# A two-layer decoder on one core: the first loads issued inside the first projection

## What is computed

```python
Q = x @ Wq; K = x @ Wk; V = x @ Wv          # 16 heads of 16
Q = _rope(Q, cos2, sin2); K = _rope(K, cos2, sin2)
scores = where(causal, Q @ K.T / 4, -inf)
x = _layernorm(x + softmax(scores) @ V @ Wo)
```

## Time and profile before

| | us |
|---|---|
| median of 3 runs | 1048.94 (1048.7 to 1051.43) |
| profiled execution | 1048.75 |
| span of the profiled execution | 1047.0 |
| mean granted clock of TensorE | 0.89 of full speed |

### The profile page before, as it was taken

One profiled execution on the slowest core, in us unless ns is written; L12 is line 12 of the kernel. 1 busy time (PEld: TensorE's weight loads), 2 busy tenths in 40 slices (PEclk: granted clock), 3 DMA queues, 4 the chain that ended last, 5 costly groups with the idle time before them and its releaser, 6 DMA issues. The chain is left out here.

```text
span 1047.0 us, 16284 instructions
## 1 busy us (share of the span) xinstructions
PE 842.6 (80%) x4838; PEld 498.2 (48%) x4838; DVE 625.5 (60%) x1971; ACT 439.3 (42%) x1422; POOL 433.7 (41%) x343
## 2 busy tenths in 40 slices
PE   1959998577475699889999998995994499999920
PEld 0445556344254344355555554883444355555510
DVE  0369994566558477668888887113665633433427
ACT  0038782355156100078888886001112155555512
POOL 0348871244026066556666664000000455565523
PEclk9989998677579699989999999998995599999975
DMA  9200000000000077620000000005911022222114
GB/s 349 108 1 1 0 1 1 0 2 1 0 1 1 17 164 171 141 81 1 2 1 2 1 1 1 1 1 212 317 74 40 16 63 71 73 69 70 51 57 144
DMA packets 30974, 60.44 MB, mean 58 GB/s; under 512 B 6465, under 2 KB 20429, under 8 KB 30032
## 3 DMA queue, kind: packets, MB, share of 16 engines
q1 hardware_dynamic: 17424, 35.99, 10.8%
q10 hardware_dynamic: 8864, 13.00, 4.4%
q0 software_dynamic: 4608, 10.50, 3.2%
HBM read 40.59 MB, written 8.39 MB: 47 GB/s over the span
## 5 line engine op out<-in xcount | busy, mean ns | idle before, releaser
L534 POOL TENSOR_TENSOR a_Pr<-a_Pr,a_rd 128x1024 f32<-128x1024 f32 x64 | 121.3, 1895 | 68.0 <-DVE a_rd L475 67.7
L507 ACT ACTIVATE a_Pr<-a_Sm,a_nm 128x257 f32<-128x257 f32 x256 | 127.3, 499 | 34.2 <-DVE a_nm L459 33.4
L459 DVE CUSTOM_DVE_ANT_0 a_Sm<-a_psS,table,NSK 128x256 f32<-128x256 f32 x256 | 107.7, 477 | 1.8 <-PE a_psS L408 1.8
L408 PE MATMUL a_psS<-KT,QT 64*128 64x256 f32 x512 | 74.2, 410 | 5.7 <-DVE a_nm L459 3.8
L1427 POOL TENSOR_TENSOR ro_in_tile<-ro_in_tile,table 128x384 fp32r<-128x384 f32 x4 | 7.0, 1746 | 173.0 <-DVE ro_in_tile L1486 173.0
L1597 POOL DMA_INDIRECT pairs<-ex_y,ti_index x48 | 49.6, 1034 | 57.5 <-ACT ex_y L1702 56.9
L1110 PE MATMUL p_ps<-p_XT,W 128*128 128x512 f32 x160 | 72.6, 612 | 0.8 <-ACT p_XT L1123 0.8
L408 PEld LDWEIGHTS a_psS<-KT,QT 64*128 64x128 f32 x512 | 45.3, 190 | 57.9 <-issue 48.6
L1140 DVE SCALAR_TENSOR_TENSOR p_T<-p_ps,BQK,table 128x512 f32<-128x512 f32 x80 | 56.4, 746 | 26.7 <-PE p_ps L1110 26.7
L1720 DVE TENSOR_TENSOR ex_a<-ex_psG,ex_sg 128x96 f32<-128x96 f32 x48 | 12.4, 258 | 99.9 <-ACT ex_sg L1690 99.9
L421 PE MATMUL a_psT<-table,a_Pr 128*128 128x128 f32 x512 | 70.8, 282 | 1.5 <-ACT a_PT L514 1.5
(11 more groups left out here) (265 smaller groups left out, 2001.2 us busy)
## 6 DMA issues: line engine op xcount, KB each, us to landing
w_in<-in_w_in SPq DMA_DIRECT2D x1, 6144.0 KB, 18.3
QT<-p_E SPq DMA_DIRECT2D x64, 64.0 KB, 2.1
QT<-p_E ACTq DMA_DIRECT2D x64, 64.0 KB, 2.1
c_in<-in_c_in SPq DMA_DIRECT2D x1, 4096.0 KB, 29.2
co_G<-pairs SPq DMA_DIRECT2D x8, 512.0 KB, 7.5
W<-in_w ACTq DMA_DIRECT2D x1, 3072.0 KB, 16.6
w_out<-in_w_out SPq DMA_DIRECT2D x1, 3072.0 KB, 43.0
KT<-p_E SPq DMA_DIRECT2D x32, 64.0 KB, 2.1
```

The costliest lines, as they stand in the source:

```text
L408: last = nc.tensor.matmul(psS[:, 2 * (t % 2) + u, qt, :], heads.q(g, n, qt), heads.k(g, n), start=True, stop=True, skip_group_check=True)
L459: nc.vector.tensor_tensor_reduce(out=Sm[:, t % 2, n, 0:S], in0=psS[:, 2 * (t % 2) + n // 2, n % 2, :], in1=mask[:, n % 2, :], scale=-scale ...
L507: nc.scalar.activation(Pr[:, t % 4, n, :], src, ACT.Exp, bias=nm[:, t % 2, n:n + 1], scale=scale if mask is None else -1.0, accum_out=den[ ...
L534: pool.tensor_tensor(p, p, rd[:, t % 2, :].unsqueeze(2).to_broadcast([P, 4, S]), ALU.mult).then_inc(normed, 1)
```

## The change

The loading block is gone. ScalarE issues the three parts of `W0` as its first instructions in the block of `project_0`, and SyncE issues all other loads in the same block, in the order of their first use: `XT`, table, `WU`, `WD`, `X`, `WO0`, `CTX`, `CT`, `HAD`, `TOK`, `GM`, `SK`, `BO1`, `W1`. The loads themselves, their sizes and the semaphores are the same.

```diff
-def project_0(nc, c, XT, W0, QT, KT, V, WU, WD, ternary, loads):
+def project_0(nc, c, XT, W0, QT, KT, V, WU, WD, ternary, loads, load_w0, load_rest):
...
         jobs = [(a, half, n) for a in range(2) for half in range(KD) for n in range(2)]
+
+        @block.sync
+        def _(sp):
+            load_rest(sp)
...
         @block.scalar
         def _(act):
+            load_w0(act)
             for t in range(NT):
                 act.wait_ge(v_made, t + 1)
...
-                with nc.Block() as block:
-                    @block.sync
-                    def _(sp):
-                        xTs = xT.rearrange("(k p) s -> p k s", p=P)
...
-                    @block.scalar
-                    def _(act):
-                        for n, m in (("q", slice(0, 2)), ("k", slice(2, 4)), ("v", slice(4, 5))):
...
+                def load_w0(act):
+                    for n, m in (("q", slice(0, 2)), ("k", slice(2, 4)), ("v", slice(4, 5))):
+                        act.dma_start(W0[:, m], w0[m].rearrange("m (k p) o -> p m k o", p=P)
+                                      ).then_inc(loads["w0" + n], 16)
+
+                def load_rest(sp):
+                    xTs = xT.rearrange("(k p) s -> p k s", p=P)
+                    for n in range(2):
+                        sp.dma_start(XT[:, :, n * 512:(n + 1) * 512],
+                                     xTs[:, :, n * 512:(n + 1) * 512]).then_inc(loads["xT%d" % n], 16)
+                    sp.dma_start(TB[:], table).then_inc(loads["consts"], 16)
+                    sp.dma_start(WU[:], wu.rearrange("(k p) o -> p k o", p=P)).then_inc(loads["wff"], 16)
+                    sp.dma_start(WD[:], wd.rearrange("(k p) o -> p k o", p=P)).then_inc(loads["wff"], 16)
+                    sp.dma_start(X[:], x.rearrange("t p d -> p t d")).then_inc(loads["x"], 16)
+                    sp.dma_start(WO0[:], wo0.rearrange("g p o -> p g o")).then_inc(loads["wo0"], 16)
+                    sp.dma_start(CTX[:], ctx.rearrange("t p d -> p t d")).then_inc(loads["ctx"], 16)
+                    sp.dma_start(CT[:], ctxT.rearrange("b (k p) s -> p (b k) s", p=P)).then_inc(loads["ctxT"], 16)
+                    sp.dma_start(HAD[:], had.rearrange("(k p) o -> p k o", p=P)).then_inc(loads["had"], 16)
+                    sp.dma_start(TOK[:], tok).then_inc(loads["tok"], 16)
+                    sp.dma_start(GM[:], gamma.to_broadcast([P, 1])).then_inc(loads["gamma"], 16)
+                    sp.dma_start(SK[:], sinks.to_broadcast([P, H1])).then_inc(loads["sinks"], 16)
+                    sp.dma_start(BO1[:], bo1.to_broadcast([P, D])).then_inc(loads["bo1"], 16)
+                    sp.dma_start(W1[:], w1.rearrange("(k p) o -> p k o", p=P)).then_inc(loads["w1"], 16)
+
+                project_0(nc, c, XT, W0, QT, KT, V, WU, WD, ternary, loads, load_w0, load_rest)
```

More of the change, by code:

```diff
@@ L1899, in decoder @@
-                project_0(nc, c, XT, W0, QT, KT, V, WU, WD, ternary, loads)
+                def load_w0(act):
[20 more added lines that the diff above has]
+                    sp.dma_start(W1[:], w1.rearrange("(k p) o -> p k o", p=P)).then_inc(loads["w1"], 16)
```

## The result

| | us |
|---|---|
| kernel before, median of 4 runs | 1050.18 (1048.7 to 1053.0) |
| changed kernel, median of 4 runs | 1035.19 (1033.94 to 1036.97) |
| ratio, 95% interval | 0.9855 (0.9827 to 0.9883) |
| changed kernel run again beside the experiments, median of 5 | 1033.84, ratio 0.985 (0.9828 to 0.9873) |
| profiled execution, its span | 1036.97, 1035.2 |

15.0 us less by the medians, where 14.9 were forecast (1034.1 us for the new time, 1035.19 measured). The ratios leave out two executions of the kernel before beside the experiments that fell in a slow state (1212.65 and 2184.34 us).

The account below looks back on a forecast made before the run. TensorE stood at the loading block's barrier until ScalarE's last issue at 21.13 us; then TensorE bounds the projection. Saving 14.9 us leaves a 1032.1 us span, 1033.9 with 1.75 around it, 1034.1 as median; 8-in-10 range 1031.5 to 1039.

Parts of the forecast that it names:

- The wait that was removed: First projection: without the loading block's barrier TensorE waits only for xT0 and w0q, first matmul at 6.85 us, saving 14.9 us.
- no row lets it be under 6.7: First projection: the first matmul's start, forecast at 6.85 us or 7.4, was said not to come before 6.7 us.
- Half-speed stretch of the first job: Job 0 of the first projection: 5.73 us to VectorE's first operation; a longer slow stretch +0.9 us, a shorter perhaps -0.5.
- Loads behind and beside the matmuls at no cost: First projection: seven loads moved to SyncE run while TensorE computes; jobs keep about 3.4 us each, nothing lost.
- The order of the loads, priced at nothing: Loads behind the table: all landed at about 35 us, next use 154 us; worst order of landings covered by over 100 us.
- SyncE's last issue: Inside the first projection: issues done at about 34 us, hidden below the block's end at 48.3 with 14 us to spare.
- The table: First projection: lands at 12.3 us, VectorE wants it at 12.6; the tightest load, but costs nothing before 14.7 us.
- The price of the rival: Late table in the first projection: landing at about 17.9 us, VectorE empties job 0 3.2 us late; 1037.3 us, chance 5%.
- The rival of the clock: Six restarts of TensorE across the stages each lose 0.9 us, 5.4 in all: 1039.5 us, chance 6%.
- The signs: Profile checks: first matmul 6.8 to 7.4 us, SyncE's issues end 30 to 36, attention's first copy 48.3, rest same within 2.
- the bound of 11: Whole kernel: prediction wrong if the 15 us are gone at the start but the end comes less than 11 us sooner.
- The rule cited from the Trainium skill: Loading block: issuing from several engines saves only usually small sequencer time; by it, removing ScalarE's ten issues would bring nothing.

Follow-up runs that it names:

- the experts' loads inside: Changed kernel with the experts' weight loads issued first thing in the domain experts' block instead of in a loading block of their own; 1032.71 us, ratio 0.9835.

## Why the prediction was right, step by step

- The wait that was removed: first matmul forecast at 6.85 us (6.7 to 7.4), found at 6.91. In the nine other profiles without the stalled barrier and with the same first loads it is at 6.43 to 6.70, so "no row lets it be under 6.7" was too narrow by up to 0.3 us. That landings would stay the same was right within 0.7 us.
- Half-speed stretch of the first job: job 0 took 5.73 us to VectorE's first operation before, 5.98 in the changed kernel's first profile, 5.70 in its second, and up to 6.80 over the experiments, 1.07 more than before where +0.9 was the bound. A gain of 0.4 of the -0.5 was seen once, with the experts' loads inside: there the first copy of attention comes 41.10 us after the first matmul, against 41.48 before. The half speed itself is read from the weight loads (0.34 us, then 0.19); the granted clock of the profile stands at 1.00 from the start of the span, while in the domain experts' stage loads of 0.34 us go with a granted clock of 0.50.
- Loads behind and beside the matmuls at no cost: (19.68 - 12.89) / 2 = 3.40 us per job with the DMA engines full, and 3.43 with twice as much to load. Right.
- The order of the loads, priced at nothing: right, by the experiment with the old one. The change's order of first use did no work here. Whether WU and WD could even come last was not run: in the changed kernel the last load, W1, has landed at 22.69 + 12.2 = 34.9 us, and WU is read at 38.06.
- SyncE's last issue was forecast at 34 us and came at 23.12. This term was mis-sized. It added the stalls of both queues one after the other, as if each issue had a stall of its own: 30.6 us for ten issues. In the kernel before, both engines stood in their issues at the same time; alone on SyncE the same ten took 17.8 us. The prediction then found its sum confirmed by the time at which the last bytes land. But an issue ends before its load has landed: W1's ended at 23.12 and landed at 34.9. It did no harm, as both are far below 48 us.
- The table: forecast to land at 12.3, 0.3 us ahead of need, with 2.3 us more until TensorE feels it. Right for the kernel as changed; in the profile with the experts' loads inside VectorE did wait for it, until 12.19, and the first copy was not later for it. The price of the rival was 3.2 us, for a landing at 17.9. In the experiment it landed at 18.90 and the copy came 6.1 us later: TensorE stood for 4.36 us, and another 2.0 came from the clock, which fell just behind this gap and which the rival had left out.
- The rival of the clock: the time of single stages changes between executions of the same program by more than the 0.9 us supposed for one restart (3.1 us in one stage), but it goes both ways. The changed kernel's second profile is 0.9 us ahead of its first at the start of cross attention and 2.0 us behind it at the start of the domain experts.
- The signs: two of them missed. SyncE's last issue was to end at 30 to 36 us. And from attention's first copy to the end it was to be the same as before within 2 us; it was 983.8 us before and 986.6 in the first profile of the changed kernel, 2.8 more, and 984.9 in the second. The first profile, 11.8 us shorter, came near the bound of 11 at which the prediction called itself wrong. The stage in two forms, which no row of the kernel before showed, made 3.1 us of this.
- What is luck: the mechanism gives 14.6 to 15.3 us at attention's first copy in the two profiles. That the medians differ by 15.0 where 14.9 was forecast is closer than the measurement can tell. The interval of the ratio goes from 12.3 to 18.2 us, and the spans of the two profiles are 11.8 and 14.1 us shorter.
- The rule cited from the Trainium skill, DMA: Bandwidth & Descriptors, section "Issuing engines are not separate DMA queues": that several issuing engines save only issue time agrees with the experiment on the old division (ratio 0.985 with two queues, 0.9855 with nearly all on one), where issue time is hidden. Its "usually small" does not hold here: WO0's issue in the changed kernel lasted 8.47 us of the 16.1 from its start to its landing.

## What to carry to other kernels

Ask of a loading block not when its data lands but when its last issue ends, and what stands behind that barrier: put only the loads of the first consumer there, or none, and let the engine with nothing else to do issue the rest. In these runs queue and order were free as long as every load landed before its need and the last issue ended before the block that holds it would; a late load costs more than its lateness if TensorE falls back to half speed behind the gap (2.0 us more here, behind a gap of 4.36).

## What the runs showed of the hardware

- An issue can hold its engine for 8 to 12 us (WO0 8.47 us in the changed kernel, 12.15 with W1 ahead). It is not the bytes issued ahead: five issues of together 15.8 MB in long rows took 0.4 to 0.5 us each at the experts' block, and WU and WD did not stall behind 6.8 MB. No single count of row pieces issued explains it either: one issue stalled at 3840, others passed at 3968 and 4480.
- One stage (domain experts) takes 72.6 to 72.8 or 75.7 to 75.9 us in different executions with the same instructions. In the long form TensorE's granted clock falls back to 0.50 some 7 us after it had risen and again near the end; the two stretches cost 1.4 and 1.7 us. In all seven long profiles the clock had risen by 4.0 us after the stage's first matmul, in all six short ones after 4.1. Single profiles must therefore be compared stage by stage before a difference of 3 us at their ends is given to an edit.
- Matmuls on a constant tile ahead of the first real one can bring the clock up in time (attention starts 1.8 us sooner: 46.14 and 46.11 in two profiles, 47.97 without), but not in each execution: with the first weights there at 5.89 us the weight loads shortened only at 6.75.
